# A macaron block on one core: the hidden bias moved from the scaling to the Silu, and a prologue in another order

## The reference

```python
x = x + 0.5 * ffn(layernorm(x))
x = x + mixer(layernorm(x))
x = x + 0.5 * ffn(layernorm(x))
```

```python
def dequant(q, scales, g):      # g = 128 rows share a row of scales
    w = (q.astype(float32) - 128.0).reshape(K // g, g, N) * scales[:, None, :]
    return w.reshape(K, N)

h = (x - mu) * rsqrt(var + EPS) * gamma + beta
y = silu(h @ dequant(fc1_q, fc1_scales, 128) + fc1_bias)
z = y @ dequant(fc2_q, fc2_scales, 128) + fc2_bias
ffn = x + 0.5 * z
```

## Time and profile before

| | us |
|---|---|
| median of three runs | 704.34 |
| lowest, highest | 703.78, 705.82 |
| the profiled execution | 704.72 |
| its span in the trace | 702.9 |

### The profile page before, as it was taken

How to read it: one execution, slowest core, us unless ns; L and a number is a source line. 1 busy time by engine, 2 the same in 40 slices (tenths; PEclk the granted TensorE clock), 3 DMA queues, 4 the chain that set the end, 5 groups by cost and what they waited for, 6 DMA issues and landing times. The chain is left out here.

```text
span 702.9 us, 13646 instructions
## 1 busy us (share of the span) xinstructions
PE 673.6 (96%) x3222; PEld 540.0 (77%) x3222; DVE 641.5 (91%) x1326; ACT 646.2 (92%) x1084; POOL 599.2 (85%) x673
## 2 busy tenths in 40 slices
PE   4999999999999999889999989999999999999997
PEld 3668888888888878667777867678888888888885
DVE  6699999999999999599999995999999999999887
ACT  4989999999999999588888887989999999999994
POOL 4799999999999999646666686989999999999974
PEclk9999999999999999999999999999999999999999
DMA  7660000000000000000000000000011000000001
GB/s 251 184 214 1 1 0 0 0 0 0 0 0 0 1 1 1 1 1 0 0 0 0 1 0 1 0 31 32 30 48 42 30 30 30 30 31 31 31 31 62
DMA packets 19963, 20.22 MB, mean 29 GB/s; under 512 B 1565, under 2 KB 19667, under 8 KB 19923
## 3 DMA queue, kind: packets, MB, share of 16 engines
q1 hardware_dynamic: 19824, 19.74, 8.7%
q10 hardware_dynamic: 98, 0.02, 0.0%
HBM read 11.37 MB, written 8.39 MB: 28 GB/s over the span
## 5 line engine op out<-in xcount | busy, mean ns | idle before, releaser
L390 POOL TENSOR_TENSOR g_lo<-g_full,g_hi 128x512 fp32r<-128x512 f32 x256 | 331.4, 1295 | 31.1 <-ACT g_hi L561 28.5
L701 DVE SCALAR_TENSOR_TENSOR z_acc<-ps_z,cols,z_acc 128x512 f32<-128x512 f32 x448 | 321.6, 743 | 28.4 <-PE ps_z L928 19.2
L928 PE MATMUL ps_fc<-h_hi,q_sb 128*128 128x512 f32 x512 | 213.3, 417 | 3.1 <-ACT ps_fc L544 2.8
L928 PE MATMUL ps_z<-g_hi,q_sb 128*128 128x512 f32 x512 | 202.5, 395 | 0.3
L559 ACT ACTIVATE g_full<-ps_fc,safe_scale 128x512 f32<-128x512 f32 x256 | 194.2, 759 | 8.8 <-PE ps_fc L928 6.7
L928 PE MATMUL ps_fc<-h_lo,q_sb 128*128 128x512 f32 x512 | 202.2, 395 | 0.0
L928 PE MATMUL ps_z<-g_lo,q_sb 128*128 128x512 f32 x512 | 200.9, 392 | 0.0
L561 ACT ACTIVATE g_hi<-ps_fc,safe_scale 128x512 fp32r<-128x512 f32 x256 | 195.6, 764 | 0.0
L544 ACT ACTIVATE ps_fc<-ps_fc,bias,ratio 128x512 f32<-128x512 f32 x192 | 156.7, 817 | 3.7 <-PE ps_fc L928 1.9
L928 PEld LDWEIGHTS ps_z<-g_hi,q_sb 128*128 128x128 f32 x512 | 96.1, 188 | 26.2 <-DVE z_acc L701 3.1
L928 PEld LDWEIGHTS ps_fc<-h_hi,q_sb 128*128 128x128 f32 x512 | 97.3, 190 | 23.7 <-ACT ps_fc L544 3.4
(11 more groups left out here) (107 smaller groups left out, 816.8 us busy)
## 6 DMA issues: line engine op xcount, KB each, us to landing
resid<-in_L_attn_x SPq DMA_DIRECT2D x15, 512.0 KB, 4.5
out_x<-resid SPq DMA_DIRECT2D x15, 512.0 KB, 2.9
q_int<-in_L_ffn_fc_q SPq DMA_DIRECT2D x4, 512.0 KB, 7.6
resid<-in_L_attn_x SPq DMA_DIRECT2D x2, 256.0 KB, 2.9
out_x<-resid SPq DMA_DIRECT2D x2, 256.0 KB, 2.5
wd_sb<-in_L_attn_Wd SPq DMA_DIRECT2D x1, 256.0 KB
wy_raw<-in_L_attn_Wy SPq DMA_DIRECT2D x2, 64.0 KB
bias_rows<-in_L_attn_by SPq DMA_DIRECT2D x1, 128.0 KB
```

Of the source, the lines that this page charges most:

```text
L390: nc.gpsimd.tensor_tensor(g_lo[:, g % 4, :], g_full[:, g % 4, :], g_hi[:, g % 4, :].bitcast(F32), ALU.subtract).then_inc(g_ready, 1)
L701: nc.vector.scalar_tensor_tensor(out=z, in0=bank_of(g, n, par), scalar=col(R_S2 + KC * g + n), in1=z, op0=ALU.mult, op1=ALU.add).then_inc( ...
L928: last = nc.tensor.matmul(out, w, v, start=start and i == 0, stop=stop and i == len(pairs) - 1, skip_group_check=not start)
```

## The change

In the order of the diff:

- `bias` is no longer divided by the scale of chunk 1 (`fold_beta` has one operation fewer), and is no longer an operand of the scalings. The scaling on ACT becomes a Copy with a scale, that on DVE a single multiplication; both wait for `ratio` instead of `bias`. Both Silus of every group get `bias` as their bias operand, and the first one waits for it.
- `rows` are turned into the first bank of `ps_fc1`, and ACT copies `cols` behind its two blocks of tile 0's `xhat`; PE turns tile 0 without waiting for `cols`.
- POOL converts the first half of q2 (a new wait for its load, ahead of tile 0's residual), ACT only the second; PE waits for each half.
- POOL normalises all four blocks of tile 1, right behind the `rsqrt` and ahead of the first `g_low`, in both feed-forward blocks; ACT's two blocks of tile 1 are gone. The counts of `xhat_half_ready` go down by one.
- DVE makes `h_lo` of chunk 0 between the two halves of q2's maximum, computes `ratio` ahead of the flag, and makes `h_lo` of chunk 1 and folds beta ahead of tile 1's statistics.
- PE does half of the second chunk's beta products ahead of the turn of the maximum.

```diff
@@ gpsimd: tile, prologue
-                        if not before and f == 1:
-                            normalise(ln0 + 1, 1, 1, halves[0], True)
+                            normalise(ln0 + 1, 1, 1, range(SUB), True)     # f == 0, behind rsqrt
...
                     prepare_columns()
+                    pool.wait_ge(q2_loaded[0], 16)
+                    nc.gpsimd.tensor_scalar(q2_sb[:, q2_halves[0], :], q2_int[:, q2_halves[0], :], -ZERO_POINT, None,
+                                            ALU.add).then_inc(q2_ready[0], 1)
                     residual(ln0, 0, 1)
@@ scalar: scale_half, silu
-                    act.wait_ge(bias_ready, 1)
+                    act.wait_ge(ratio_ready, 2)
...
-                nc.scalar.activation(bank, bank, ACT.Identity, bias=bias[:, f:f + 1],
-                                     scale=ratio[:, f:f + 1]).then_inc(scaled_on_act, 1)
+                nc.scalar.activation(bank, bank, ACT.Copy, scale=ratio[:, f:f + 1]).then_inc(scaled_on_act, 1)
...
+                if type(ff) is int and ff == 0 and g == 0:
+                    act.wait_ge(bias_ready, 1)
...
-                nc.scalar.activation(g_full[:, g % 4, :], bank, ACT.Silu, scale=scale)
+                nc.scalar.activation(g_full[:, g % 4, :], bank, ACT.Silu, bias=shift_of, scale=scale)
...
-                nc.scalar.activation(g_hi[:, g % 4, :], bank, ACT.Silu, scale=scale).then_inc(g_hi_ready, 1)
+                nc.scalar.activation(g_hi[:, g % 4, :], bank, ACT.Silu, bias=shift_of,
+                                     scale=scale).then_inc(g_hi_ready, 1)
@@ scalar: tile, prologue
-                        if not before and f == 1:
-                            normalise(ln0 + 1, 1, 1, halves[1], xhat_half_ready)
...
                     normalise(ln0, 0, 0, halves[1], xhat_half_ready)
+                    act.wait_ge(rows_turned, 1)
+                    nc.scalar.activation(cols[:, :], ps_fc1[:, 0, 0:ROWS], ACT.Copy).then_inc(cols_ready, 1)
+                    act.wait_ge(cols_ready, 1)
                     convert_q1(0)
...
-                    for k in range(KC):
-                        act.wait_ge(q2_loaded[k], 16)
-                    nc.scalar.activation(q2_sb[:, :, :], q2_int[:, :, :], ACT.Copy,
-                                         bias=-ZERO_POINT).then_inc(q2_ready, 1)
+                    act.wait_ge(q2_loaded[1], 16)
+                    nc.scalar.activation(q2_sb[:, q2_halves[1], :], q2_int[:, q2_halves[1], :], ACT.Copy,
+                                         bias=-ZERO_POINT).then_inc(q2_ready[1], 1)
@@ vector: scale_half, prologue, fold_beta
-                nc.vector.tensor_scalar(bank, bank, ratio[:, f:f + 1], bias[:, f:f + 1], ALU.mult,
-                                        ALU.add).then_inc(scaled_on_dve, 1)
+                nc.vector.tensor_scalar(bank, bank, ratio[:, f:f + 1], None, ALU.mult).then_inc(scaled_on_dve, 1)
...
                         largest_of(KC + k, q2_int[:, part, :].rearrange("p g d -> p (g d)"), q2_loaded[k])
+                        if k == 0:
+                            lower_h(ln0, ff0, 0, 0)
...
-                    lower_h(ln0, ff0, 0, 0)
+                    dve.wait_ge(ratio_ready, 1)
+                    nc.vector.tensor_tensor(ratio[:, :], cols[:, R_S1:R_S1 + FC], inverse[:, :],
+                                            ALU.mult).then_inc(ratio_ready, 1)
                     find_width()
...
+                    lower_h(ln0, ff0, 0, 1, ps_tr2)
+                    dve.wait_ge(beta_done, KC)
+                    fold_beta(1)
                     dve.wait_ge(x_loaded[1], 16)
                     statistics(1)
                     variance(ln0 + 1, 1)
-                    dve.wait_ge(beta_done, KC)
-                    fold_beta(1)
-                    lower_h(ln0, ff0, 0, 1, ps_tr2)
...
-                nc.vector.tensor_tensor(bias[:, :], bias[:, :], inverse[:, :], ALU.mult).then_inc(
@@ tensor: prologue
-            pe.wait_ge(cols_ready, 1)
...
+            pe.wait_ge(q1_ready, KC)
+            beta_products(1, q1_sb, groups=range(0, FC // 2))
             pe.wait_ge(largest_found, 5)
             nc.tensor.transpose(ps_z[0:1, 0, 0:P], largest[:, 4:5], ident[:, :]).then_inc(largest_turned, 1)
-            pe.wait_ge(q1_ready, KC)
-            beta_products(1, q1_sb).then_inc(beta_done, 1)
+            beta_products(1, q1_sb, groups=range(FC // 2, FC)).then_inc(beta_done, 1)
```

More of the change, by code:

```diff
@@ L169, in macaron_kernel @@
         q1_ready = sem("q1_ready")
-        q2_ready = sem("q2_ready")
+        q2_ready = [sem(f"q2_ready{k}") for k in range(KC)]
         beta_ready = sem("beta_ready")
@@ L259, in share @@
         def share(ln, ff0):
-            return ln - (NT - 2) if ff0 else ln + 1
+            return ln - NT if ff0 else ln
         def mix_bank(t, par, half):
@@ L477, in mixer_tile @@
                 if behind:
-                    rsqrt(t + (NT + 2), par, behind == 1, 0 if before else NT + 2)
+                    rsqrt(t + (NT + 2), par, behind == 1, 0 if before else NT + 1)
                 for c in range(KC) if behind else ():
@@ L503, in _ @@
             nc.scalar.activation(silu_table[:, :], minus_half[:, 0, 0:1], ACT.Silu)
-            act.wait_ge(rows_turned, 1)
-            nc.scalar.activation(cols[:, :], ps_tr2[:, 0:ROWS], ACT.Copy).then_inc(cols_ready, 1)
-            act.wait_ge(cols_ready, 1)
             def convert_q1(k):
@@ L554, in silu @@
             def silu(ff, g, par):
-                step, bank, scale = FC * ff + g, ps_fc1[:, g % 4, :], safe_scale[:, g:g + 1]
+                step, bank = FC * ff + g, ps_fc1[:, g % 4, :]
+                scale, shift_of = safe_scale[:, g:g + 1], bias[:, g:g + 1]
+                if type(ff) is int and ff == 0 and g == 0:
+                    act.wait_ge(bias_ready, 1)
                 act.wait_ge(fc1_done, step + 1)
                 wait(act, g_ready, FC * ff + (g - 3))
-                nc.scalar.activation(g_full[:, g % 4, :], bank, ACT.Silu, scale=scale)
+                nc.scalar.activation(g_full[:, g % 4, :], bank, ACT.Silu, bias=shift_of, scale=scale)
                 wait(act, fc2_done, 2 * step - 6)
-                nc.scalar.activation(g_hi[:, g % 4, :], bank, ACT.Silu, scale=scale).then_inc(g_hi_ready, 1)
+                nc.scalar.activation(g_hi[:, g % 4, :], bank, ACT.Silu, bias=shift_of,
+                                     scale=scale).then_inc(g_hi_ready, 1)
             def turn_out(t, par, c, outs=(0, 1), bank=ps_tr):
@@ L678, in scale_half @@
                 if type(ff) is int and ff == 0 and f == SCALED_ON_DVE[0]:
-                    dve.wait_ge(bias_ready, 1)
+                    dve.wait_ge(ratio_ready, 2)
                 bank = ps_fc1[:, f % 4, :]
-                nc.vector.tensor_scalar(bank, bank, ratio[:, f:f + 1], bias[:, f:f + 1], ALU.mult,
-                                        ALU.add).then_inc(scaled_on_dve, 1)
+                nc.vector.tensor_scalar(bank, bank, ratio[:, f:f + 1], None, ALU.mult).then_inc(scaled_on_dve, 1)
             def lower_h(ln, ff, par, c, bank=ps_tr):
@@ L763, in feed_forward @@
                     nc.vector.reciprocal(inverse[:, :], safe_scale[:, :]).then_inc(ratio_ready, 1)
-                    lower_h(ln0, ff0, 0, 0)
+                    dve.wait_ge(ratio_ready, 1)
+                    nc.vector.tensor_tensor(ratio[:, :], cols[:, R_S1:R_S1 + FC], inverse[:, :],
+                                            ALU.mult).then_inc(ratio_ready, 1)
                     find_width()
-                    dve.wait_ge(ratio_ready, 1)
-                    nc.vector.tensor_tensor(ratio[:, :], cols[:, R_S1:R_S1 + FC], inverse[:, :], ALU.mult)
+                    lower_h(ln0, ff0, 0, 1, ps_tr2)
+                    dve.wait_ge(beta_done, KC)
+                    fold_beta(1)
                     dve.wait_ge(x_loaded[1], 16)
@@ L789, in fold_beta @@
                 last.then_inc(beta_scaled, 1)
-                dve.wait_ge(beta_scaled, 3 * turn - 2)
+                dve.wait_ge(beta_scaled, 2 * turn - 1)
                 nc.vector.tensor_reduce(out=bias[:, :], in_=beta_terms[:, :, :], axis=AX.X,
                                         op=ALU.add).then_inc(beta_scaled, 1)
[L793 to L796, removed]
-                nc.vector.tensor_tensor(bias[:, :], bias[:, :], inverse[:, :], ALU.mult).then_inc(
+                dve.wait_ge(beta_scaled, 2 * turn)
+                nc.vector.tensor_tensor(bias[:, :], bias[:, :], cols[:, R_B1:R_B1 + FC], ALU.add).then_inc(
                     bias_ready if turn == 1 else wide_bias_ready, 1)
@@ L841, in prepare_wide @@
                     dve.wait_ge(q1_ready, KC)
-                    dve.wait_ge(q2_ready, 1)
+                    for k in range(KC):
+                        dve.wait_ge(q2_ready[k], 1)
                     chunks = [(q1_low[:, k, :], q1_sb[:, k, :], q1_int[:, k, :]) for k in range(KC)]
@@ L912, in _ @@
             pe.wait_ge(rows_loaded, 16 * 9)
```

(12 more changed lines are left out.)

## The result

The changed kernel takes 720.55 us (median of 6 runs, 719.30 to 721.61), the kernel before 704.06 beside it (6 runs, 703.53 to 705.82): a ratio of 1.0226, 95% interval 1.0208 to 1.0243. The prediction was 718.0, range 713.5 to 725.0. The profiled run of after took 721.08 us, its span is 719.2.

The account below looks back on a forecast made before the run. PE was taken to bound the kernel by 2.4% of a tile ahead of ACT, with ACT becoming the bound. +14.9 - 1.0 - 0.5 = +13.4 us on the profiled 704.7 gave 718.1, adjusted to 718; range 713.5 to 725.

Parts of the forecast that it names:

- The operand's price: On ACT, each operand column adds about 0.093 us, a Silu's second too: Silu 0.66 us, net +0.93 us a tile.
- Who becomes the bound: In the steady tile, ACT at 16.99 us passes PE's 16.45 and becomes the bound.
- ACT's slack: In a steady tile before, ACT's one gap of 0.39 us is all its slack; 28 gaps sum to 11.2 us.
- the period of 17.0: Sign of being right: a steady tile period of 17.0 us, with no 0.39 gap on ACT.
- the 17.2 with ACT still waiting: Sign of being wrong: a tile period of 17.2 us or more with ACT still waiting, its gaps kept.
- The loop of 1.42 us against 1.89: Steady tile: scaling, PE's second half, Silu take 1.42 us while ACT issues 1.89, so ACT's gaps vanish.
- the rival that ACT keeps its gaps: Steady tile: PE's waits return as ACT's, the full 26.0 us stay, 729 us; with half, 723; 9% above 725.
- The first head: First block's start up to the steady tiles: the new order gains 1.0 us if POOL no longer idles.
- The sum of POOL's idle times: First head: POOL idles 3.36 us; minus 1.3 for a later rsqrt and 1.08 for added blocks leaves 1.0 gained.
- The half of q2: First head: POOL's conversion of q2's first half takes 2.2 us, ending with the residual three us ahead of the rsqrt.
- The stall of tile 1: End of the first head: PE's 1.63 us wait at 47.52 for a DVE addition stays; ends 0 and 1.6 saved.
- Between the blocks: Second block's head: two blocks leave ACT's queue, dearer Silus take some back, 0.4 to 0.5 us gained.

Follow-up runs that it names:

- The operand alone: The kernel before with both Silus taking the bias and the scalings on ACT and DVE without it, nothing else: 723.38 us, ratio 1.0265.
- the order alone: The changed kernel with the bias put back into the scalings: 702.62 us, ratio 0.9977 against the kernel before.
- The half dose: The changed kernel with the bias left out of the g_hi Silu, so only g_full takes it: 703.9 us, ratio 0.9984 against the kernel before.
- the normalise alone: The kernel before with POOL normalising all four blocks of tile 1 ahead of the first g_lo, ACT none: 702.91 us, ratio 0.9975.
- the rest of the order alone: The new order with tile 1 normalised as before, half on POOL and half on ACT, and the bias in the scaling: 704.71 us, ratio 1.0000.
- the run with the late variance: The kernel before with DVE's variance of the next tile but one moved from group 4 to group 6: 700.92 us, ratio 0.9957.

## Why the prediction held, point by point

- **The operand's price: right.** 0.093 us for each [128,1] operand, on a Silu's second one too. The Trainium skill (ScalarE: Activation LUTs, section What ACT_TABLE_LOAD costs) says about 93 ns for each; the step from 0.57 to 0.66 agrees.
- **Who becomes the bound: right.** ACT, in every steady tile. With no gap, with one, and with 8 matmuls a tile fewer, its ends come 17.17 us apart. The operand alone costs 2.65%, the order alone gains 0.23%.
- **ACT's slack: the mis-sized term.** The prediction read ACT's work from start to start, 16.45 - 0.39 = 16.06. But the ends ran late: the earlier trace rows has a Silu of 0.68 us at 66.61, after the gap, and one of 0.86 at 65.07, at the tile's end. These 0.18 us are work too, and the gap had to give them back: 16.06 + 0.18 = 16.24, and 16.24 + 0.93 = 17.17, which is the period measured. The half dose makes 16.24 + 0.19 = 16.43, on the threshold, as measured. The slack was 0.21 us a tile and not 0.39; over 28 tiles the difference is 28 x 0.18 = 5.0 us, of which 4.4 show, since part of the lag isn't given back by the end of a block: the Silu that closes the 14 tiles lasts 1.02 and 1.21 us where the one that opens them lasts 0.78, 0.24 and 0.43 more. So the period of 17.0 that the prediction named as a sign of being right came out as 17.17, with a gap of 0.15 us on the mean, just under the 17.2 with ACT still waiting that it named as a sign of being wrong. The row hinted at it: ACT idle for 0.10 us a tile, where the starts leave 0.39.
- **The loop of 1.42 us against 1.89: wrong for a steady tile.** It took the scaling's 0.76 us from the earlier trace rows. With the lag a scaling takes 1.24 in the timeline above, and the loop from its start to the Silu is 218.56 - 216.51 = 2.05 us, 0.16 more than ACT's own 1.89: the gap comes back. So the rival that ACT keeps its gaps was true in part, 0.18 of 0.39, though not because PE is slow.
- **The first head: right by size for the order (1.16 measured alone, 1.0 predicted), for another reason in part.** The sum of POOL's idle times didn't set it: the wait of 0.77 for ACT stayed with either part of the order, and of the 1.16 the normalise alone gives 0.70 and the other moves 0.45. Tile 1's rsqrt and turn came where they were forecast, 18.4 and 22.8:

```profile
11.04 2.78 POOL L468 TENSOR_SCALAR q_sb<-q_int 128x1024 fp32r<-128x1024 int32 x1 [0.58 <-DMA q_int<-in_L_ffn_fc_q]
13.80 2.16 POOL L380 TENSOR_SCALAR resid<-resid,res_scale,shift 128x256 f32<-128x256 f32 x4
18.50 1.67 POOL L355 TENSOR_TENSOR rstd<-var_terms,minus_half 128x8 f32<-128x8 f32 x1 [2.53 <-DVE neg_mean L673]
20.72 2.16 POOL L369 TENSOR_SCALAR xhat<-resid,rstd,shift 128x256 f32<-128x256 f32 x4
...
22.94 0.66 PE L921 MATMUL ps_tr<-ident,xhat 128*128 128x128 f32 x4 [0.56 <-POOL xhat L369]
```

  The half of q2 took 2.78 us, not 2.2; the residual behind it ended at 15.96, 2.5 us ahead of the rsqrt, so that cost nothing. But the later rsqrt was no price either, as the rest of the order alone shows.
- **The stall of tile 1: wrong.** It was left where it was, with 0 to 1.6 us as bounds. In after it is nearly gone, 0.41 us on PE where it was 1.63:

```profile
43.49 0.80 DVE L667 TENSOR_SCALAR var_terms<-mean_var 128x4 f32<-128x4 f32 x1
44.21 0.16 DVE L669 TENSOR_SCALAR var_terms<-mean_var 128x4 f32<-128x4 f32 x1
44.28 0.56 DVE L673 TENSOR_SCALAR neg_mean<-mean_var 128x4 f32<-128x4 f32 x1
44.74 0.68 DVE L709 SCALAR_TENSOR_TENSOR resid<-ps_tr,resid 128x512 f32<-128x512 f32 x1
...
45.56 0.63 PE L985 MATMUL ps_tr<-ident,z_acc 128*128 128x128 f32 x4 [0.41 <-DVE resid L709]
```

  The neg_mean that took 1.79 us now takes 0.56, as it falls otherwise between POOL's g_lo. The dearer Silus did that and not the order: with the order alone that neg_mean takes 1.78 us and tile 1 lasts 18.66 us (from the second Silu of group 4 to the next tile's), 2.2 more than the tile behind it, as before; with the operand alone it takes 0.56, and the tile lasts 17.79, 0.8 more than the one behind it. On ACT the gap ahead of the first Silu of group 5 went from 2.56 to 0.79 us, -1.77; with the order's -1.16 that is -2.93, and the -1.96 measured leaves about +1.0 for the dearer Silus of the first one and a half tiles, which the prediction had left out of this head. (With the operand alone the same sum gives +1.4: -0.40 measured, and -1.77 from the stall.)
- **Between the blocks: the same stall, once more**, 0.74 us now. How much of the -1.35 is the change's can't be said from one pair of profiles: with the same steady tile this stretch took 178.86 us before, and 176.79, 178.25 and 178.76 in the runs of the order, the normalise and the rest.

## What to carry to other kernels

Where two engines are within a few per cent of each other, a few operands decide which is the bound: count them by instruction and tile, since moving one bias from six scalings to sixteen Silus cost more than ten times what the reordered prologue gained (18.7 us against 1.6). Read an engine's work from end to end as well as from start to start; if durations grow while it never pauses, as they did here, the growth over a period is work, and the slack is that much smaller. A short instruction that takes ten times its usual duration beside another engine's long one is worth moving away from whatever waits behind it, here 3.0 to 3.7 us for one constant.

## What the runs showed of the hardware

- ACT's instructions, issued without a pause, ended 6 to 7 ns later each than their starts alone would make them: the duration rose from 0.92 to 1.08 us over the 25 steps from 237.00 to 252.67. Signals came at the ends. The lag went up to 0.6 us (a Silu with both operands at 1.37 us, after a long pause 0.78) before ACT's wait for PE stopped it. What holds the ends back wasn't tried.
- DVE's small instructions of the variance, over four elements, took 0.16 to 0.17 us alone and up to 1.79 beside POOL's subtraction of 1.27; in the run with the late variance, 2.37 beside one of 2.54. The Trainium skill (SBUF — State Buffer, section Who interferes with whom) describes DVE and GpSimd sharing a port pair, held by one at a time. The 1.79 us that end with POOL's subtraction, and the 3.0 to 3.7 us gained by moving them, agree with that; that it is the ports, no run here shows.
- On POOL 1024 elements from int32 took 2.78 us and 1024 float elements, in four instructions, 2.16.
